# Second attention: one score tile in every fifth unit gets its exponential from VectorE, by a float32 polynomial and exponent bits

## The reference

```python
q = (x @ wq + bq).reshape(B, Sq, H, D).transpose(0, 2, 1, 3)
k = (y @ wk + bk).reshape(B, -1, H, D).transpose(0, 2, 1, 3)
v = (y @ wv + bv).reshape(B, -1, H, D).transpose(0, 2, 1, 3)
scores = jnp.einsum('bhqd,bhkd->bhqk', q, k) / jnp.sqrt(jnp.asarray(D, x.dtype))
attn = jax.nn.softmax(scores, axis=-1)
out = jnp.einsum('bhqk,bhkd->bhqd', attn, v)
return out.transpose(0, 2, 1, 3).reshape(B, Sq, E) @ wo + bo
```

## Time and profile before

| | us |
|---|---|
| median of the runs | 1857.36 |
| the profiled execution, its own time | 1853.31 |
| its span | 1851.5 |
| PE busy in the span | 1582.9 |
| ACT busy | 1373.1 |
| DVE busy | 854.8 |
| POOL busy | 169.9 |

### The profile page before, as it was taken

One profiled execution on the slowest core, in us unless ns is written; L12 is line 12 of the kernel. 1 busy time (PEld: TensorE's weight loads), 2 busy tenths in 40 slices (PEclk: granted clock), 3 DMA queues, 4 the chain that ended last, 5 costly groups with the idle time before them and its releaser, 6 DMA issues. The chain is left out here.

```text
span 1851.5 us, 22757 instructions
## 1 busy us (share of the span) xinstructions
PE 1582.9 (85%) x8261; PEld 603.4 (33%) x8261; DVE 854.8 (46%) x2331; ACT 1373.1 (74%) x1441; POOL 169.9 (9%) x154
## 2 busy tenths in 40 slices
PE   6789788898998993776789999999999999985996
PEld 4463354554554552533211111111111111113442
DVE  7768999999999997473400000000000000003223
ACT  5737687888887874313289999999999999982332
POOL 4840211111111101000000000000000000000000
PEclk8869899999999996787689999999999999997998
DMA  3430968979769679350000004000500000003000
GB/s 103 144 117 0 184 150 177 202 155 210 174 151 230 152 179 241 78 152 7 18 1 1 1 1 63 13 1 1 75 1 1 1 1 1 1 1 98 0 1 12
DMA packets 69263, 143.41 MB, mean 77 GB/s; under 512 B 21993, under 2 KB 40642, under 8 KB 68218
## 3 DMA queue, kind: packets, MB, share of 16 engines
q0 software_dynamic: 13616, 75.73, 20.5%
q1 hardware_dynamic: 55098, 65.30, 13.2%
q10 hardware_dynamic: 432, 0.85, 0.1%
HBM read 52.65 MB, written 13.99 MB: 36 GB/s over the span
## 5 line engine op out<-in xcount | busy, mean ns | idle before, releaser
L1936 ACT ACTIVATE ex<-ps 128x1536 f32<-128x1536 f32 x536 | 721.9, 1494 | 6.0 <-PE ps L1890 6.0
L1905 PE MATMUL ps<-ex,V 128*9 128x512 f32 x3200 | 419.8, 597 | 0.5 <-ACT ex L1936 0.4
L850 PE MATMUL ps<-K,qst 128*128 128x512 f32 (+1 forms) x832 | 392.9, 604 | 30.7 <-ACT srow L920 20.7
L1890 PE MATMUL ps<-Q,K 52*128 52x512 bf16 (+1 forms) x1632 | 322.8, 385 | 39.1 <-ACT ex L1936 34.2
L1946 DVE COPY o<-ps 9x512 f32<-9x512 f32 x32 | 22.0, 687 | 714.2 <-PE ps L1909 713.5
L1051 DVE MAX8 cand<-srow 128x8 f32<-128x200 f32 (+1 forms) x1024 | 318.7, 359 | 8.7 <-ACT srow L920 8.6
L1011 DVE SCALAR_TENSOR_TENSOR both<-srow,top,both 128x1536 f32<-128x1536 f32 (+1 forms) x128 | 239.4, 1870 | 21.2 <-ACT both L937 21.0
L920 ACT COPY srow<-ps 128x1024 f32<-128x1024 f32 (+1 forms) x224 | 205.1, 924 | 46.1 <-PE ps L850 45.7
L937 ACT ACTIVATE both<-srow,shift 128x1536 f32<-128x1536 f32 (+1 forms) x128 | 209.4, 1638 | 23.2 <-DMA both<-both 21.8
L1890 PEld LDWEIGHTS ps<-Q,K 52*128 52x128 bf16 (+1 forms) x1632 | 60.7, 94 | 448.1 <-ACT ex L1936 433.1
L850 PEld LDWEIGHTS ps<-K,qst 128*128 128x128 f32 x832 | 150.8, 198 | 166.5 <-issue 116.1
(11 more groups left out here) (333 smaller groups left out, 1087.2 us busy)
## 6 DMA issues: line engine op xcount, KB each, us to landing
both<-both POOLq DMA_DIRECT2D x69, 768.0 KB, 8.9
v_ring<-v_rows SPq DMA_DIRECT2D x84, 256.0 KB, 6.3
both<-both POOLq DMA_DIRECT2D x23, 898.0 KB, 13.1
K<-k_parts SPq DMA_DIRECT2D x48, 204.0 KB
k_parts<-kl SPq DMA_DIRECT2D x12, 384.0 KB, 2.6
V<-v_rows SPq DMA_DIRECT2D x4, 900.0 KB, 6.7
v_rows<-v1g SPq DMA_DIRECT2D x12, 288.0 KB, 3.8
srow<-v_rows SPq DMA_DIRECT2D x1, 3200.0 KB, 17.5
```

The lines of the kernel that those rows point to most:

```text
L850: last = M.matmul(ps[:, BANK_OF[item] + b, 0:c1 - c0], qst[:, h, :], K0[:, c0:c1], start=True, stop=True)
L1890: last = M.matmul(out, K1[rows_, quad % 2, hh // 2, keys], Q1[rows_, 4 * quad + hh, tb * TB:(tb + 1) * TB], start=True, stop=True, tile_po ...
L1905: last = M.matmul(out, V1[:, quad % 2, g, VW * j:VW * j + VW], ex1[:, slot(w, 4 * g + j), :], start=g == 0, stop=False, tile_position=(0, ...
L1936: C.activation(ex1[:, s:s + NBANK, :], ps[:, b:b + NBANK, :], ACT.Exp)\
```

## The change

Every fifth unit, from unit 6 on, is an own unit (12 in a pass: 6, 11, ..., 61). Its third tile is left out of ACT's exponential, which then covers 1024 columns. DVE makes that tile's exponential with ten instructions (`power_of_two`): the score, already in units of log 2, is held above -118, rounded to a whole number by adding a large constant, the rest goes through a polynomial of degree five, and the whole number, shifted into the exponent bits, is multiplied in. The result goes to one of 8 slots of a new tile `power`. The scores are now scaled by 1 / ln 2 (`SC1`), so ACT's exponential gets the factor `LN2`, and the limit `EXP_RANGE` is scaled too.

PE leaves the own tiles out of their groups (three matmuls in place of four) and multiplies them in batches of four (`own_values`), after the scores and the group of units 27, 47 and 66. PE's scores now also wait for DVE's first instruction on the own tile of two units before or earlier (`own_read`), the batches wait for four finished tiles (`powered`), and DVE's last instruction on a tile waits until the slot was used (`power_used`). DVE's copies of a pass's sums are now made at the beginning of the next pass's list.

```diff
-EXP_RANGE = 60.0
+LOG2E = float(np.log2(np.e))
+LN2 = float(np.log(2.0))
+EXP_RANGE = 60.0 * LOG2E
...
-        SC1 = float(DH1) ** -0.5
+        SC1 = float(DH1) ** -0.5 * LOG2E
...
+        BATCH = 4
+        power = sb(b8, "power", [P, 2 * BATCH, TB])
+        score, whole_, part, poly = (sb(b8, name, [P, TB]) for name in ("score", "whole_part", "part", "poly"))
...
+        EVERY, FIRST_U, BATCHES = 5, 6, 3
+        OWN = [FIRST_U + EVERY * i for i in range(BATCH * BATCHES)]
+        LATE_AT = {OWN[BATCH * (b + 1) - 1] + (EVERY if b == BATCHES - 1 else EVERY + 1): b for b in range(BATCHES)}
+        OWN_TILE = {NBANK * u + NBANK - 1: i for i, u in enumerate(OWN)}
...
                     if w * NU + u >= 2:
                         pe.wait_ge(S("exped1"), w * NU + u - 1)
+                        if own_before(w * NU + u - 1):
+                            pe.wait_ge(S("own_read"), own_before(w * NU + u - 1))
...
                     for j in range(4):
+                        if 4 * g + j in OWN_TILE:
+                            continue
...
+                def own_values(w, b):
+
+                    quad = w // NB
+                    pe.wait_ge(S("powered"), w * len(OWN) + BATCH * (b + 1))
+                    for i in range(BATCH * b, BATCH * (b + 1)):
+                        n = NBANK * OWN[i] + NBANK - 1
+                        g, j = divmod(n, 4)
+                        last = M.matmul(ps[32 * j:32 * j + VW, 6 + w % 2, :], V1[:, quad % 2, g, VW * j:VW * j + VW],
+                                        power[:, (w * len(OWN) + i) % (2 * BATCH), :], start=False, stop=False,
+                                        tile_position=(0, 32 * j))
+                    last.then_inc(S("power_used"), 1)
...
+                        if u in LATE_AT:
+                            own_values(w, LATE_AT[u])
...
-                        C.activation(ex1[:, s:s + NBANK, :], ps[:, b:b + NBANK, :], ACT.Exp)\
-                            .then_inc(S("exped1"), 1)
+                        n = NBANK - 1 if u in OWN else NBANK
+                        C.activation(ex1[:, s:s + n, :], ps[:, b:b + n, :], ACT.Exp, scale=LN2).then_inc(S("exped1"), 1)
...
+                def power_of_two(w, i):
+
+                    u, slot_ = OWN[i], (w * len(OWN) + i) % (2 * BATCH)
+                    dve.wait_ge(S("scored1"), w * NU + u + 1)
+                    V.tensor_scalar(score[:, :], ps[:, bank(w, NBANK * u + NBANK - 1), :], LOW2, None, ALU.max)\
+                        .then_inc(S("own_read"), 1)
+                    dve.wait_ge(S("own_read"), w * len(OWN) + i + 1)
+                    dchain(V.tensor_scalar(whole_[:, :], score[:, :], ROUND2, None, ALU.add))
+                    dchain(V.scalar_tensor_tensor(part[:, :], whole_[:, :], ROUND2, score[:, :], ALU.subtract, ALU.subtract))
+                    dchain(V.tensor_scalar(poly[:, :], part[:, :], POWER[5], None, ALU.mult))
+                    for k in (4, 3, 2, 1):
+                        dchain(V.scalar_tensor_tensor(poly[:, :], poly[:, :], POWER[k], part[:, :], ALU.add, ALU.mult))
+                    bits = whole_[:, :].bitcast(I32)
+                    dchain(V.tensor_scalar(bits, bits, 23, None, ALU.logical_shift_left))
+                    done = w * BATCHES + i // BATCH
+                    if done >= 2:
+                        dve.wait_ge(S("power_used"), done - 1)
+                    V.scalar_tensor_tensor(power[:, slot_, :], poly[:, :], POWER[0], whole_[:, :], ALU.add, ALU.mult)\
+                        .then_inc(S("powered"), 1)
...
+                for w in range(NPASS):
+                    if w:
+                        read_sums(w - 1)
+                    for i in range(len(OWN)):
+                        power_of_two(w, i)
+                read_sums(NPASS - 1)
```

More of the change, by code:

```diff
@@ L1839, in program, with own_before @@
         assert NTILE % NBANK == 0 and NSLOT % NBANK == 0
+        EVERY, FIRST_U, BATCHES = 5, 6, 3
+        OWN = [FIRST_U + EVERY * i for i in range(BATCH * BATCHES)]
+        LATE_AT = {OWN[BATCH * (b + 1) - 1] + (EVERY if b == BATCHES - 1 else EVERY + 1): b for b in range(BATCHES)}
+        OWN_TILE = {NBANK * u + NBANK - 1: i for i, u in enumerate(OWN)}
+        assert max(LATE_AT) < NU and len(LATE_AT) == BATCHES and NBANK * FIRST_U >= 4
+        LOW2, ROUND2 = -118.0, ROUND + 127.0
+        POWER = (1.0000000716546564, -0.6931469670638629, 0.2402211972393386, -0.055507132749627305,
+                 0.009675541330686871, -0.0013276471518916786)
+        def own_before(k):
+            w, u = divmod(k, NU)
+            return w * len(OWN) + sum(1 for o in OWN if o < u)
         def last_tile(g):
@@ L1935, in _, with read_sums @@
                         s, b = slot(w, NBANK * u), bank(w, NBANK * u)
-                        C.activation(ex1[:, s:s + NBANK, :], ps[:, b:b + NBANK, :], ACT.Exp)\
-                            .then_inc(S("exped1"), 1)
+                        n = NBANK - 1 if u in OWN else NBANK
+                        C.activation(ex1[:, s:s + n, :], ps[:, b:b + n, :], ACT.Exp, scale=LN2).then_inc(S("exped1"), 1)
             @block.vector
             def _(dve):
-                dve.wait_ge(S("o1_zero"), 1)
-                for w in range(NPASS):
+                def read_sums(w):
                     quad, tb = divmod(w, NB)
@@ L1947, in _ @@
                                       ps[32 * j:32 * j + VW, 6 + w % 2, :]).then_inc(S("o1_read"), 1)
+                def power_of_two(w, i):
[16 more added lines that the diff above has]
+                        .then_inc(S("powered"), 1)
+                dve.wait_ge(S("o1_zero"), 1)
+                for w in range(NPASS):
[4 more added lines that the diff above has]
+                read_sums(NPASS - 1)
     q1s.close()
```

## The result

The changed kernel's median is 1857.48 us (1851.49 to 1864.05, 20 runs), the kernel before in the same comparison 1854.15 us (1849.72 to 1858.78, 20 runs): a ratio of 1.002, 95% interval 1.001 to 1.0029, so 3 to 4 us slower (1.9 to 5.4 us by the interval). Forecast were 4 us more, on another median of the kernel before (1857.36), hence 1861.

A forecast was written before the change was run, and what follows sets the result against it. The prediction took ACT as the bound, with PE close behind; PE's extra groups outweighed ACT's cut, 91.3 us a pass against 90.8, +4 us on 1857.4, hence 1861 us (slower, 0.53), range 1842 to 1878.

The forecast's parts named there:

- The bound: In the second attention's stage, ACT paces units at 1.344 us; PE leaves room of only 3.4 us a pass.
- free slot: PE's time in each fourth unit, which has no value matmuls: 0.84 us, able to shrink to 0.63.
- ACT's cut: Exponentials of 1024 columns instead of 1536 in 12 of 67 units: 0.43 us each, 41 us in all.
- the walk: Pass stepped through start by start, each the latest of its causes: 90.81 us for the kernel before, against 90.76 measured.
- PE's batches: Three extra groups of value matmuls a pass on PE, 0.98 us each: +2.93 us, nothing taken away.
- X: Time of DVE's ten-instruction chain per own tile: between 6.4 and 6.7 us, taken as 6.5.
- Rival C: DVE's chain becomes the bound from X = 6.72 us; at 6.8, 92.4 us a pass and 1870 us; chance 0.18.
- The third batch's wait: PE's wait for finished tiles at unit 66, 7.2 us needed against 7.2 available: put at 0.1 us a pass.
- D: Rival: PE's second wait costs 0.05 us in each unit with value matmuls, 1.5 us a pass, 1873 us; chance 0.10.
- The sum: The changed pass takes 91.3 us against 90.8: +0.5 us a pass, +4 us in all.
- PE's account: Changed pass added up on PE from value groups, scores, 16 free slots (three at 1.01 us) and waits: 91.3 us.
- Eight times: Step from +0.5 us a pass to +4 us for the whole stage.

The follow-up runs named there:

- e2: Changed kernel with full 1536-column exponentials in own units, the first bank read three times: 1871.74 us, ratio 1.0089 to the kernel before.
- e1: Changed kernel without the 24 batches of own-tile value matmuls, PE still waiting for finished tiles: 1841.17 us, ratio 0.9925 to the kernel before.
- e6: Changed kernel with both full exponentials in own units and no batches of own-tile value matmuls: 1856.16 us, ratio 1.0006 to the kernel before.
- e3: Changed kernel with the polynomial's first product made twice on DVE, chain 6.89 us instead of 6.43: 1870.63 us, ratio 1.0091 to the kernel before.
- e5: Changed kernel with own units at 5, 10, ..., 60 and batches in units 26, 46, 66: 1852.16 us, ratio 0.998 to the kernel before.
- e4: Kernel before, with DVE taking all four tiles of groups 4, 19, 34, returned in units 30, 50, 62 that have no group: 1841.49 us, ratio 0.9915.
- e8: As e4, but the three groups return in units 31, 51, 63 beside another group: 1856.77 us, ratio 1.0015 to the kernel before.

## Why the prediction was right

*The bound.* ACT was it, with PE close behind: e2 shows that ACT still counts, e1 that PE does. The step that carried the forecast, that a free slot shrinks from 0.84 us to 0.63 and no further, stands in the trace: in the slot at 1257.89 the second unit's three weights are loaded at 1258.53, 0.64 us after the first's.

*ACT's cut.* 0.43 us a unit was right: the exponential of an own unit ends 0.92 us after the one ahead of it, others 1.34 where ACT sets the pace. Of its 5.1 us a pass 2.0 reach the pass, by e2 and e6; the walk had 2.1. That the factor costs nothing was right too (e6), but the working has a slip: 1450 ns lie 7 ns above 1443, not 11.

*PE's batches.* They are 2.93 us of PE's work a pass, of which the prediction's walk let 91.3 - 88.7 = 2.6 reach the pass; by e1 it is 2.34. The difference is of size and not of kind: a batch behind a group starts 0.86 us after it and not 0.98 (1253.04 to 1253.90), which is 0.23 us a pass. The rule of the Trainium skill (TensorE: Matmul & The Clock Gate, Measured speedup vs the span model), some 4 ns for each further matmul of a packed group, holds: a group of three is followed after 0.971 to 0.975 us, one of four after 0.978, so that one matmul fewer saves 3 to 7 ns.

*DVE's chain.* X was set at 6.5 and is 6.43, 6.35 as a pace. The unseen integer shift took the one-input 0.43 us; I had put 0.55. The table of the Trainium skill (VectorE: DVE Perf Modes, The perf-mode tier table) gives that rate for float32 and does not name the shift. Rival C needs 0.36 us more a tile by its working: e3 gave it 0.46 and it came, with 92.59 us a pass and 1870.63 in all, where the prediction had 92.4 and 1870 for 6.8 us a tile.

*The third batch's wait,* put at 0.1 us a pass, costs nothing (0.65 us behind unit 66's scores with it and without). D costs nothing either (e6 and the spacing of PE's groups).

*The sum* had +0.5 us a pass; measured are +0.34. PE's account gave 91.3, and less the 0.23 above it is 91.1, the pass that was measured. *Eight times* that was the step with a size that did not hold: the stage grew by 1.3 us, not by 4, since the first and the last pass did not grow. The medians differ by 3.3 us (1.9 to 5.4 by the interval), so some 2 us of that are not found in the stage, of which there is one profiled execution of each kernel. That 3.3 came so near to the forecast 4 is in part luck; where the other 2 us come from is open.

*What it got wrong:* it foresaw 1861 because it was set on a median of three runs, 1857.36; twenty runs give the kernel before 1854.15. And PE's account had three wide slots (1.01 us) in which PE has caught up, which the trace bears out, but did not draw the conclusion: such a slot holds idle time of PE, so that a batch placed there costs 0.50 us and not 0.86 (e5; e4 against e8 shows the same for whole groups).

## What to carry to other kernels

Work taken off the bound is worth only what the next engine leaves free (here 2.0 us of 5.1 a pass), and how little that is could be read from one slot in the timeline before anything was built. Matmuls that run side by side in column groups were paid by the group here: take a whole group away or none, and put it back where a unit has none (e4, 0.85% faster, with twelve tiles moved as well). For an engine with a chain that comes back in part of a pass, set the intervals between its starts against the time of that part, not its busy share against the pass (e3). And a gain or loss per pass times the number of passes is not yet the stage's: look at the first and the last.

## What the runs showed of the hardware

A group of float32 value matmuls directly behind another of the same kind starts 0.86 us after it, where scores in bfloat16, or the 32-row group of line 1934, start 0.97 to 0.98 after (in the timeline above, and 1218.18 to 1219.16 at a seam). The 32-row group is float32 too, so the type alone does not make the difference. An integer shift of 512 columns on VectorE took 0.43 us, 2048 columns 1.23, as the one-input float32 instructions did. An instruction of VectorE that waits for the one ahead starts 34 ns after the end of its record; one that does not started 0.08 us before its forerunner's record ended (1140.57 + 0.69 against 1141.18).
